# A channel-attention kernel on one core: weight halves made by other engines, loads and first-pair statistics reordered, and the folded weights M evacuated in straight pieces first

## The reference

```python
g = group_norm(x, 32 groups, eps=1e-5)             # per image, 6 channels by 2304 positions
xt = g.reshape(b, c, n).transpose(0, 2, 1)
q, k, v = split(xt @ w_qkv)                        # w_qkv 192 x 576, 8 heads of 24 channels
q, k = each divided by its norm over the n positions (floor 1e-12); k = k * temperature
attn = softmax(k^T q)                              # 24 x 24 for each head and image
out = (v @ attn^T) @ w_out + b_out
return x + out
```

## Time and profile before

| what | value |
|---|---|
| median of three runs | 384.58 us |
| the profiled execution: its own time | 383.51 us |
| its span, first to last instruction | 381.7 us |
| mean granted TensorE clock | 0.976 |
| TensorE busy (matmul) | 332.8 us |
| VectorE busy | 285.3 us |
| ScalarE busy | 234.5 us |
| GpSimd busy | 148.7 us |
| DMA, mean rate over the span | 177 GB/s |

### The profile page before, as it was taken

One profiled execution on the slowest core, in us unless ns is written; L12 is line 12 of the kernel. 1 busy time (PEld: TensorE's weight loads), 2 busy tenths in 40 slices (PEclk: granted clock), 3 DMA queues, 4 the chain that ended last, 5 costly groups with the idle time before them and its releaser, 6 DMA issues.

```text
span 381.7 us, 9324 instructions
## 1 busy us (share of the span) xinstructions
PE 332.8 (87%) x3724; PEld 231.9 (61%) x3724; DVE 285.3 (75%) x668; ACT 234.5 (61%) x409; POOL 148.7 (39%) x131
## 2 busy tenths in 40 slices
PE   0068477989999899989998999989998999999695
PEld 0056336865778467855786577846685578764452
DVE  5987867986698669886797769876988665359664
ACT  1098289845996299727985499719973798510200
POOL 0179547503960178114940297016811394001000
PEclk9999958999999999999999999999999999999899
DMA  7999800004993289615990499327971562044756
GB/s 243 365 300 234 212 0 3 2 3 155 299 301 117 84 277 313 199 63 129 343 330 8 145 303 320 104 85 248 320 219 45 179 204 75 2 142 133 222 175 198
DMA packets 30826, 67.73 MB, mean 177 GB/s; under 512 B 5504, under 2 KB 12096, under 8 KB 30784
## 3 DMA queue, kind: packets, MB, share of 16 engines
q1 hardware_dynamic: 30544, 66.56, 55.1%
q10 hardware_dynamic: 240, 0.59, 0.6%
HBM read 29.38 MB, written 28.31 MB: 151 GB/s over the span
## 4 chain that ended last, share of the span: by engine, by line
PE 53%; DVE 18%; ACT 12%; issue 12%; POOL 2%; DMA 1%; SPq 0%; ACTq 0%; POOLq 0%; DVEq 0%
PE u_ps L890 26%; PE g_ps L890 11%; PE s_ps L890 10%; DVE bnst L693 6%; ACT tok L549 4%; ACT h_sb L524 3%; DVE x_sb L817 3%; ACT xn L518 2%; PE u_ps L939 2%; PE u_ps L940 2%; ACT mh L571 2%; DMA x_sb<-in_x_dram 1%; DVE ml L783 1%; DVE q L798 1%; DVE mv L703 1%
## 5 line engine op out<-in xcount | busy, mean ns | idle before, releaser
L455 POOL TENSOR_TENSOR l_sb<-xn,h_sb 128x768 f16<-128x768 f32 x63 | 103.8, 1650 | 55.8 <-ACT h_sb L524 55.5
L817 DVE SCALAR_TENSOR_TENSOR x_sb<-u_ps,bias,x_sb 128x384 f32<-128x384 f32 x144 | 85.3, 612 | 22.8 <-PE u_ps L890 22.6
L890 PE MATMUL g_ps<-tok 128*128 128x64 f16 (+1 forms) x864 | 85.5, 239 | 4.1 <-ACT tok L549 3.5
L518 ACT ACTIVATE xn<-x_sb,rb 128x768 f32<-128x768 f32 x63 | 63.6, 1021 | 37.2 <-POOL rb L467 37.2
L549 ACT COPY tok<-u_ps 128x384 f32<-128x384 f32 x144 | 64.6, 484 | 16.6 <-PE u_ps L942 16.4
L890 PE MATMUL u_ps<-h_sb,ml 128*128 128x384 f16 (+1 forms) x336 | 73.9, 329 | 0.0
L890 PEld LDWEIGHTS g_ps<-tok 128*128 128x128 f16 x864 | 55.8, 98 | 29.4 <-ACT tok L549 7.5
L693 DVE BATCH_NORM_STATS2 bnst<-x_sb 128x6 f32<-128x384 f32 x144 | 69.7, 544 | 3.5 <-DMA x_sb<-in_x_dram 3.1
L524 ACT ACTIVATE h_sb<-x_sb,rb 128x768 f16<-128x768 f32 x63 | 64.4, 1022 | 0.0
L939 PE MATMUL u_ps<-id,h_sb 128*128 128x128 f16 x288 | 48.4, 222 | 5.5 <-DVE l_sb L683 5.5
L461 POOL TENSOR_TENSOR grs<-gvar,minus_half 128x3 f32<-128x3 f32 x8 | 7.1, 883 | 110.6 <-DVE gvar L726 110.6
(11 more groups left out here) (142 smaller groups left out, 568.4 us busy)
## 6 DMA issues: line engine op xcount, KB each, us to landing
x_sb<-in_x_dram SPq DMA_DIRECT2D x48, 384.0 KB, 5.4
out_dram<-x_sb SPq DMA_DIRECT2D x48, 384.0 KB, 3.0
out_dram<-x_sb SPq DMA_DIRECT2D x48, 192.0 KB, 2.8
x_sb<-in_x_dram SPq DMA_DIRECT2D x45, 192.0 KB, 5.4
hl<-h_sb SPq DMA_DIRECT2D x48, 96.0 KB, 2.9
hl<-l_sb SPq DMA_DIRECT2D x48, 96.0 KB, 2.8
x_sb<-in_x_dram ACTq DMA_DIRECT2D x3, 192.0 KB, 4.2
w<-in_L_conv_w_qkv_dram SPq DMA_DIRECT2D x1, 288.0 KB
```

The costliest lines, as they stand in the source:

```text
L455: nc.gpsimd.tensor_tensor(l_sb[:, par, t, cols], xn[:, c % XN_RING, :], h_sb[:, par, t, cols], ALU.subtract).then_inc(l_ok, 1)
L518: nc.scalar.activation(xn[:, c % XN_RING, :], xcol(q, t, g * GW, GW), ACT.Identity, bias=rb[:, par, 1, t:t + 1], scale=rb[:, par, 0, t:t + ...
L817: V.scalar_tensor_tensor(out=xs, in0=block_ps(n), scalar=bias[:, t:t + 1], in1=xs, op0=ALU.add, op1=ALU.add).then_inc(out_ok, 1)
L890: return nc.tensor.matmul(dst, lhs, rhs, start=start, stop=stop, skip_group_check=True)
```

## The change

- **Loads.** `w0`, `w1` (twice) and `wo` are issued before the loads of pair 1, on `c_in` (count 64). Mask, biases and temperatures stay before those of pair 2, on a semaphore `c_small`.
- **High weights by ScalarE.** Six `scalar.mul` ahead of the first `first_high` replace six GpSimd instructions.
- **Low weights by GpSimd.** `low_constants` makes four low halves, each by a multiplication into `xn` and a subtraction, with `temp4` after them. VectorE keeps only `wol` ("wo").
- **The first split.** The last third of pair 0 gets its high half in three pieces of 768 columns in place of six of 384; two high halves (8 and 11) are made by VectorE from the value in `s_ps`. Seven statistics pieces of pair 1 go between VectorE's values and low halves (`FIRST_BN`), seven behind.
- **First tables.** In `FIRST_VEC_B` "gram" comes before "var"; "wv" comes after "stats"; `FIRST_ACT_B` begins with chunk 0 and only the value of chunk 1.
- **M.** `high_m` makes the two straight pieces of `mh1` from `s_ps` first, tells VectorE, waits for them, and copies them to the other partitions from SBUF. `low_m` is cut into "m0" (after slot 11) and "m1" (after slot 13); `BN_A` puts six pieces before m0 and two between m0 and m1. Result block 0 waits for the copies too.

```diff
-VEC_A = {0: ["soft_in"], 3: ["soft_out"], 7: ["v"], 11: ["m"], 17: ["stats"]}
+VEC_A = {0: ["soft_in"], 3: ["soft_out"], 7: ["v"], 11: ["m0"], 13: ["m1"], 17: ["stats"]}
-FIRST_ACT_A = {1: [6, 7], 2: [8], 3: [9, 10], 4: [11], 5: [12, 13], 6: [14], 7: [15, 16], 8: [17]}
-FIRST_ACT_B = [0, 1, "t0", "t1", "t2", 2, 3, 4, 5, "x6", "x7"]
+FIRST_ACT_A = {1: [6, 7], 2: [9], 3: [10], 4: [12], 5: [13], 6: [14]}
+FIRST_ACT_B = [0, "x1", "t0", "t1", "t2", "h1", 2, 3, 4, 5, "x6", "x7"]
-FIRST_VEC_A = {17: ["bn"] * 10 + ["wv"] + ["bn"] * 4 + ["stats", "low0", "low1"]}
-FIRST_VEC_B = {0: ["var", "gram", "z", "low2", "low3", "t0", "t1"], 1: ["t2", "bn", "bn", "low4", "low5", "norms", "spread", "bn", "bn"]}
-BN_A = {1: 2, 5: 4, 9: 4, 13: 4}
+FIRST_VEC_A = {17: ["bn"] * 7 + ["stats", "wv"]}
+FIRST_VEC_B = {0: ["gram", "var", "z", "t0", "t1"], 1: ["t2", "bn", "bn", "wo", "norms", "spread", "bn", "bn"]}
+FIRST_BN = (0, 2, 2, 2, 1)
+BN_A = {1: 2, 5: 4, 9: 6, 11: 2}
-LAST_VEC_A = {0: ["m"]}
+LAST_VEC_A = {0: ["m0", "m1"]}
...
+                if q == 1:
                     sp.dma_start(w0[:, :], w_qkv[0:P, :]).then_inc(c_in, 16)
...
+            def lows(terms, base, length):
+                ch = Chain(pool, low_ok, base, length)
+                for dst, src, hi, at in terms:
+                    ch.then(nc.gpsimd.tensor_scalar(at, src, W_SCALE, None, ALU.mult))
+                    ch.then(nc.gpsimd.tensor_tensor(dst, at, hi, ALU.subtract))
...
+            def high_constants():
+                act.wait_ge(c_in, 64)
+                act.wait_ge(fills, 1)
+                qk = slice(0, 2 * C)
+                nc.scalar.mul(wh0[:, :], w0[:, qk], W_SCALE)
+                nc.scalar.mul(wh1[:, :], w1[:, qk], W_SCALE)
+                for b in (0, 1):
+                    r = slice(C1 * b, C1 * b + C1)
+                    nc.scalar.mul(wmh[r, b, :], w1[r, qk], W_SCALE)
+                nc.scalar.mul(woh[:, :, 0:C], wo[:, :, :], W_SCALE)
+                nc.scalar.mul(woh[:, :, C:C + P], wo[:, :, 0:P], W_SCALE).then_inc(high_ok, 1)
...
                 act.wait_ge(m_mm, 2 * q + 2)
                 for b in (0, 1):
-                    for i in (0, 1):
-                        ins = nc.scalar.mul(mh1[C1 * i:C1 * i + C1, b, :], s_ps[C1 * b:C1 * b + C1, 1, 0:C], M_EVAC)
+                    r = slice(C1 * b, C1 * b + C1)
+                    ins = nc.scalar.mul(mh1[r, b, :], s_ps[r, 1, 0:C], M_EVAC)
+                ins.then_inc(mh_ok, 1)
+                act.wait_ge(mh_ok, 3 * q + 2)
+                for b in (0, 1):
+                    ins = nc.scalar.copy(mh1[C1 * (1 - b):C1 * (1 - b) + C1, b, :], mh1[C1 * b:C1 * b + C1, b, :])
                 ins.then_inc(mh_ok, 1)
...
+                if BY_VECTOR[i] in HIGH_BY_VECTOR:
+                    V.tensor_copy(h_sb[:, 0, t, cols], s_ps[:, i % 2, 0:BW]).then_inc(h0_vec, 1)
+                    dve.wait_ge(h0_vec, HIGH_BY_VECTOR.index(BY_VECTOR[i]) + 1)
...
                         first_value(i)
                         first_value(i + 1)
+                        pieces(now, FIRST_BN[i // 2])
                         first_low(i)
                         first_low(i + 1)
...
                     pe.wait_ge(ml_ok, 2 * q + 2)
+                    pe.wait_ge(mh_ok, 3 * q + 3)
```

More of the change, by code:

```diff
@@ L248, in preact_attention @@
         high_ok = sem("high_ok")
+        low_ok = sem("low_ok")
+        temp_ok = sem("temp_ok")
+        wo_ok = sem("wo_ok")
+        h0_vec = sem("h0_vec")
         wv_ok = sem("wv_ok")
@@ L283, in preact_attention, with high_count @@
         STAT, GVAR, NORM, DIAG, SOFT, ATTN = 6, 4, 2, 3, 5, 6
+        def high_count(k):
+            if k < WHOLE:
+                return k + 1 - sum(n <= k for n in HIGH_BY_VECTOR)
+            return WHOLE - len(HIGH_BY_VECTOR) + (k - WHOLE) % 3 + 1
         def need(eng, s, value):
@@ L428, in first_split @@
                     pool.wait_ge(xn0_pool, n + 1)
[L429 removed]
+                    pool.wait_ge(h0_ok, high_count(k))
                     nc.gpsimd.tensor_tensor(l_sb[:, 0, t, cols], at, h_sb[:, 0, t, cols], ALU.subtract).then_inc(l0_pool, 1)
[L432 to L439, removed]
[L440 to L446 removed]
@@ L529, in first_high @@
                 t, part = MINIS[k]
-                cols = slice(part * BW, part * BW + BW)
-                nc.scalar.activation(h_sb[:, 0, t, cols], xcol(0, t, part * BW, BW), ACT.Identity,
+                cols = slice(part * BW, part * BW + (BW if k < WHOLE else GW))
+                nc.scalar.activation(h_sb[:, 0, t, cols], xcol(0, t, cols.start, cols.stop - cols.start), ACT.Identity,
                                      bias=rb[:, 0, 1, t:t + 1], scale=rb[:, 0, 0, t:t + 1]).then_inc(h0_ok, 1)
+            def high_constants():
[9 more added lines that the diff above has]
+                nc.scalar.mul(woh[:, :, C:C + P], wo[:, :, 0:P], W_SCALE).then_inc(high_ok, 1)
             def split(q, par, what):
@@ L643, in copy_bias, with out_weights @@
             def copy_bias():
[L645 removed]
+                dve.wait_ge(c_small, 16 * (4 + NH))
                 V.tensor_copy(bias[:, 2:3], bias[:, 0:1])
[L648 to L660 removed]
+            def out_weights():
+                dve.wait_ge(high_ok, 1)
+                for cols, n in ((slice(0, C), C), (slice(C, C + P), P)):
+                    V.scalar_tensor_tensor(out=wol[:, :, cols], in0=wo[:, :, 0:n], scalar=W_SCALE, in1=woh[:, :, cols],
+                                           op0=ALU.mult, op1=ALU.subtract).then_inc(wo_ok, 1)
             def value_weights():
@@ L667, in value_weights @@
                 dve.wait_ge(wv_ok, 1)
-                low(wvl[:, :, :], wv_ps, wvh[:, :, :]).then_inc(wv_ok, 1)
+                V.scalar_tensor_tensor(out=wvl[:, :, :], in0=wv_ps, scalar=W_SCALE, in1=wvh[:, :, :],
+                                       op0=ALU.mult, op1=ALU.subtract).then_inc(wv_ok, 1)
             def first_value(i):
@@ L860, in step @@
                             pieces(now, 1)
-                        elif what[0:3] == "low":
-                            low_constant(int(what[3]))
                         elif what == "wv":
@@ L877, in step @@
                             pieces(later, 1)
-                        elif what[0:3] == "low":
-                            low_constant(int(what[3]))
+                        elif what == "wo":
+                            out_weights()
                         elif gram:
@@ L986, in gram_weights @@
                         pe.wait_ge(wv_ok, 2)
-                        pe.wait_ge(high_ok, 8)
-                    pe.wait_ge(set_v, 2 if ready else 1)
+                        pe.wait_ge(high_ok, 1)
+                    pe.wait_ge(low_ok, 4 if ready else 2)
                 if not ready:
```

72 lines of the change are left out of this document (38 added, 34 removed).

## The result

The changed kernel takes 373.55 us (median of 4 runs, 372.27 to 374.76) against 384.63 us for the kernel before (4 runs, 384.32 to 385.0): ratio 0.9709, 95% interval 0.9689 to 0.9729, 11.1 us saved. The prediction, 373.5 us, holds. The profiled execution took 374.76 us, the longest of the four, with a span of 372.8 us.

The account below looks back on a forecast made before the run. In the steady part VectorE's late end of phase A was taken to bound, making TensorE wait. Steady 6.9, tail 2.3 and head 1.85 us sum to 11.05: 372.5 us for the profiled execution, 373.5 median, range 371.0 to 377.5.

Parts of the forecast that it names:

- The steady part: Six ordinary steps: VectorE ends phase A sooner, TensorE's stall at the group sums shrinks; 6.9 us, bounds 4 and 7.2.
- ScalarE's copies: Steady steps: two SBUF copies and a 0.1 us wait replace two multiplications, hidden; at worst 0.3 us a step.
- the first term: Last step: two fewer multiplications ahead of m1 shorten TensorE's 2.19 us wait for `ml` by 0.66 us.
- the second: Tail: after the shorter wait of 1.5 us the clock stays up, saving 1.6 us.
- Likelier near 16: Head: the four weight loads land by 18.7 at the latest, likelier near 16, so the scale at 19.4 isn't delayed.
- The Gram: Head: end of the Gram 0.3 us sooner, bounds 0.3 later and 0.5 sooner.
- GpSimd's weights: Head: eight weight instructions of at most 0.92 us on GpSimd, ending near 41.5.
- The clock in the head: Before pair 1's phase A: TensorE idles 3 to 5 us, the clock falls and takes back 1.7 us, bounds 0 and 2.7.
- 1.85 of head: Head net: first `tok` of pair 1 3.55 us sooner, less 1.7 us for the clock.
- (c): Rival: the head gains nothing and the tail's clock falls as before; 377.0 us, chance 0.14.
- (d): Rival: another wait (casts of `q`, `tok` copies) takes half the steady gain; 377.0 us, chance 0.13.
- (e): Rival: slower or the same, as late loads of pieces 14 to 17 hold up m1 and block 0; chance 0.05.
- (b): Rival: the clock does not fall before pair 1's phase A, 1.7 us better; 371.8 us, chance 0.14.

Follow-up runs that it names:

- order_only: Kernel before with only VectorE's new phase A order (six pieces, m0, two pieces, m1), ScalarE's four multiplications left as they were: 377.73 us, ratio 0.9822.
- straight_only: Kernel before with straight pieces of mh1 first and copies behind, old piece order, m0 and m1 together after slot 11: 378.38 us, ratio 0.9834.
- head_only: Changed kernel with its M part undone, leaving only loads, weights, first split and first tables changed: 381.5 us, ratio 0.9921 against the kernel before.
- no_first_bn: Changed kernel with all fourteen statistics pieces of pair 1 behind pair 0's low halves, none between them: 373.54 us, ratio 0.9715 to the kernel before.
- after_again: Changed kernel run again unchanged as a yardstick: 372.52 us, ratio 0.9698 against the kernel before.
- after_third: Changed kernel run unchanged once more, in another group, as a yardstick: 373.03 us, ratio 0.9687 against the kernel before.
- tail_warm: Changed kernel plus 4 and 8 unread TensorE matmuls in the last step, the 8 where it waits for `ml`: 372.83 us, ratio 0.9687 to kernel before.
- wo_late: Changed kernel with `w_out` loaded with pair 2 on its own semaphore and its high half made after slot 14: 373.41 us, ratio 0.9706 to kernel before.
- all_warm: Changed kernel with the edits of wo_late, warm and tail_warm together: 372.37 us (5 runs), ratio 0.9681 against the kernel before.
- warm: Changed kernel plus 16, 12 and 14 unread matmuls where TensorE stands in the head: 372.14 us, ratio 0.9683 against the kernel before.
- warm_wo: Changed kernel with the edits of wo_late and warm joined: 372.98 us, ratio 0.9682 against the kernel before.

## Why the prediction was right, and where its terms were not

**The steady part: right in mechanism and size.** 6.9 us were predicted and 6.7 measured, the step 40.4 and 40.45. "Stats" at 0.5 us before block 0 is the 0.50 of the timeline. The reason "VectorE idles before both low halves" is confirmed from both sides, by order_only (all of the gain without the straight pieces) and by straight_only (VectorE still waits 0.79 us, TensorE still 0.45 us). One statement was too generous to the change: the straight pieces are not needed for the steady gain. I had them carry a part of the 2.0 us by which "stats" ends sooner; with the new order the wait that they shorten is covered by two pieces already.

**ScalarE's copies: hidden, as said.** From `mh0` to the `tok` behind the block it was 1.98 us and is 2.05 now, 0.07 longer where I took 0.1. Two copies take 0.71 us, so about 0.35 each. The estimate of 0.25 us by the Trainium skill ("ScalarE: Activation LUTs", "What ACT_TABLE_LOAD costs") took off 93 ns of overlap from the 0.35 us that 186 ns and 0.833 ns an element give for 192 columns. The trace agrees with the 0.35 for one copy (0.349 us) and shows no overlap between these: two take 0.71. The 0.33 of the nearest row was the better one.

**The tail: the first term right, the second only sometimes (mis-sized where the clock falls).** The wait went from 2.19 to 1.54 us, 0.65 where 0.66 was predicted. The 1.6 us for the clock came in six of nine profiles; with 2.19 us of waiting (before, order_only, head_only) the clock fell in all three. The argument was that 1.5 us is shorter than an idling of 2.08 us that the clock had stood through the earlier trace rows. Three falls after 1.54 us refute it as a rule: the length of the last idling alone does not decide.

**The head: three terms mis-sized.** (1) "Likelier near 16" for the weights was wrong: they were there at 16.7 to 17.9. At 17.1 and 17.2 that costs nothing (head_only, no_first_bn), at 17.8 some 0.3 us (the changed kernel). The start after 19.5 was one of the signs that I had named for a wrong prediction; it came by 0.9 us, but 0.6 of that is pair 0's own scale, which was ready 0.6 us later than before. Whether the weights' loads delay it or it scatters by itself was not tested. (2) The Gram was to end 0.3 us sooner. It ended 1.2 us later in the first profile and 0.2 sooner in after_again. The pieces among the low halves cost TensorE a wait of 0.98 us, and by its profile no_first_bn, without them, brings the first value only 0.1 us later, counted from the first high half. `parts`, foreseen near 40, ended at 42.7 and in after_again at 41.2; the casts still ended last, so that cost nothing. (3) GpSimd's weights were put at 0.92 us an instruction and an end near 41.5. The multiplications take 1.17 us and the last subtraction ends at 44.7; the scale waits for neither, since `temp` was ready before the variance. The trace of before had the price: its GpSimd multiplication of `w` into `wh` (L439, 128x384) takes 1.17 us, and the 0.92 was that of a subtraction. The first value came at 46.1 to 48.0, not 45.9. From there to `tok` it took 14.0 us (14.1 predicted).

**The clock in the head: right place, uncertain size, and one fall left out.** The fall before phase A came in five of the seven profiles of the changed head that have no unread matmuls in it. It cost 2.2 and 2.1 us in changed and after_again and 1.1 or 1.2 in head_only, after_third and tail_warm, against 12.0 us with full clock (predicted 1.7, bounds 0 to 2.7). In wo_late and no_first_bn it didn't come, and the stretch took 12.0 us. The sum also had the scores end at 53.6 at full clock. In all seven the clock fell already around the idling of some 3.45 us before them; the scores ran at half clock as in the kernel before, and ended near 58 in the changed kernel. Before, that held up the product for M; now nothing waits for it, and it makes the idling before phase A shorter (2.90 us in the changed kernel, 3.85 in head_only, where the clock was back sooner).

**Why the sum fits so well.** 11.05 us against 11.1 is in part luck. The steady part and the first tail term, 7.6 us, stand as worked out. The rest, 3.5 us, was to be 1.85 of head and 1.6 of clock in the tail; the medians give 3.2 for the head alone (head_only) and an uncertain tail. That the slip of the head's start and the clock's falls, which differ from execution to execution, come out at the 3.5 us is luck. And the first profile shows 8.9 us, not 11.1, since the new profiled execution is the longest of its four and the old one the shortest of those shown. Of the rivals, (c) and (d) at 377.0 are out. So is (e): in the steady steps VectorE waits once for a load, 0.30 us at 199.54. What (b) says, no fall before phase A, is seen in the profiled executions of wo_late and no_first_bn; they took 372.77 and 373.22 us, not 371.8, and in both the tail's clock fell instead. A slip in the range: "by the steady bound", 0.3 us, its lower end would be 371.5, not 371.0.

## What to carry to other kernels

When an engine idles before an instruction and stands late behind it, look first whether work that it has to do anyway can go into the gap: here a reordering of six and two statistics pieces gave the whole steady gain, and the restructured evacuation added 0.65 us once, in the tail, with a shorter idling through which the clock stood in six of nine profiles. Judge a head from several executions, not one: here its start shifted by 0.9 us and its end, by the clock, by 2 us, which is as much as the edits bring. Work placed among instructions that feed another engine is not free because its own engine idled there; in the profile of no_first_bn moving it back costs 0.1 us at the first value, and the medians can tell no difference.

## What the runs showed of the hardware that was not expected

- The granted clock falls in one execution and stays in another after the same idling (1.54 us, fallen in three of nine). Before phase A it fell around an idling of 2.90 us in the changed kernel and stood through one of 3.31 us in wo_late. The Trainium skill, "TensorE: Matmul & The Clock Gate", section "HAM oscillation — how this bites in real kernels", tells of idling that throttles the array again; the traces agree that it does, but none of them lets one foretell it for a gap of this length.
- The clock explains less of the time than the profile suggests. Executions of the changed kernel with a mean clock of 0.984 and 0.985 took 372.2 and 374.51 us, and two of all_warm with 1.00 took 372.37 and 373.36. The 13 executions of the changed kernel have a median of 372.98, the 14 of warm, warm_wo and all_warm together 372.5 (from different groups, so this is no test). With a mean clock of 0.99 or more the three kernels with unread matmuls still spread from 371.57 to 373.67 us. The 0.9 us at the first high half could be a part of it, but that was seen only in profiles and not isolated; it stays open.
- The granted clock in the rows is not the whole speed of TensorE at the start. In the changed kernel it reads 1.00 from 23 to 26 us, yet matmuls of 128 columns follow each other there every 0.107 us, and from 27 us on every 0.055. So part of the half speed in the head is missing from the mean clock of a run.
- Some very short VectorE instructions took longer while GpSimd worked beside them: the 128x6 cast of 0.17 us took 0.45 and 0.77 us in the fence above, and a 96x8 one 1.39 us in warm, while the 128x384 pieces keep their 0.5 us. Others of 0.17 us beside the same GpSimd work were not stretched (41.49 in that fence). The coincidence is seen; its cause wasn't tried. VectorE and GpSimd of warm:

```profile
57.69 1.39 DVE L771 TENSOR_SCALAR n<-n 96x8 f32<-96x8 f32 x1
```

```profile
57.40 1.65 POOL L474 TENSOR_TENSOR l_sb<-xn,h_sb 128x768 f16<-128x768 f32 x1 [0.16 <-ACT h_sb L543]
```
